# An attention factorization machine on one core: SyncE's row fetches and a placed field go, 16 tiles per quad are looked up by matmul, gathers skip ids clamped to the last row

## The reference, cut to what matters

```python
emb = jax.vmap(lambda tbl, idx: tbl[idx], in_axes=(0, 1), out_axes=1)(embed_tables, sparse)
bi = emb[:, FIRST, :] * emb[:, SECOND, :]
a = jax.nn.relu(jnp.einsum('bpd,dh->bph', bi, att_w_w) + att_w_b)
scores = jnp.einsum('bph,ho->bpo', a, att_d_w) + att_d_b
att_weight = jax.nn.softmax(scores, axis=1)
att_out = jnp.sum(att_weight * bi, axis=1)
out = jax.nn.sigmoid(jnp.concatenate([att_out, dense], axis=-1) @ fin_w + fin_b)
```

## Time and profile before

| what | value |
|---|---|
| time, median of 3 runs | 478.24 us (478.12 to 480.02) |
| span of the profiled execution | 755.4 us |
| PE busy / instructions | 489.4 us / 2788 |
| DVE busy / instructions | 419.0 us / 692 |
| ACT busy / instructions | 118.3 us / 218 |
| POOL busy / instructions | 343.8 us / 357 |
| TensorE clock granted, mean | 0.837 |

### The profile page before, as it was taken

How to read it: one execution, slowest core, us unless ns; L and a number is a source line. 1 busy time by engine, 2 the same in 40 slices (tenths; PEclk the granted TensorE clock), 3 DMA queues, 4 the chain that set the end, 5 groups by cost and what they waited for, 6 DMA issues and landing times.

```text
span 755.4 us, 9968 instructions
## 1 busy us (share of the span) xinstructions
PE 489.4 (65%) x2788; PEld 175.7 (23%) x2788; DVE 419.0 (55%) x692; ACT 118.3 (16%) x218; POOL 343.8 (46%) x357
## 2 busy tenths in 40 slices
PE   2853102136686888737696898647687989999516
PEld 0321000012222233312232233212222224433102
DVE  6943003047475656444485666254476666899616
ACT  4211000003011123000011132000012132013114
POOL 6777777624745441744564541744564640000000
PEclk9985555559888899958898999868898999999958
DMA  7532521201211111111221110121221210000000
GB/s 234 120 18 13 99 13 12 13 3 9 13 8 12 8 10 33 12 8 10 11 11 10 10 10 4 13 37 9 11 12 9 12 10 2 2 2 2 0 1 1
DMA packets 15495, 15.60 MB, mean 21 GB/s; under 512 B 8177, under 2 KB 14161, under 8 KB 15057
## 3 DMA queue, kind: packets, MB, share of 16 engines
q0 software_dynamic: 11296, 5.81, 14.3%
q1 hardware_dynamic: 3488, 8.38, 3.1%
q10 hardware_dynamic: 656, 0.79, 0.4%
HBM read 14.93 MB, written 0.02 MB: 20 GB/s over the span
## 4 chain that ended last, share of the span: by engine, by line
SPq 59%; issue 38%; DVE 1%; PE 1%; DMA 1%; ACT 1%; ACTq 0%
SPq L411 51%; SPq L407 7%; DMA index<-look_index 0%; PE sums_s L515 0%; DVE ring L855 0%; PE sums_f L501 0%; PE first L491 0%; ACT score L685 0%; SPq L380 0%; DVE neg_max_early L891 0%; DMA emb_placed<-tables 0%; SPq L385 0%; ACT second_s L627 0%; ACT hidden L614 0%; PE back_s L538 0%
## 5 line engine op out<-in xcount | busy, mean ns | idle before, releaser
L441 POOL DMA_INDIRECT emb<-tables,rows x308 | 294.0, 955 | 261.0 <-DVE emb_t L831 164.6
L476 PE MATMUL looked_own<-look_parts,onehot 128*128 128x448 bf16 x735 | 178.8, 388 | 119.3 <-issue 75.3
L855 DVE TENSOR_TENSOR ring<-emb_t,turned 128x512 f32<-128x512 f32 (+9 forms) x180 | 193.9, 1114 | 3.4
L476 PE MATMUL back_s<-look_parts,onehot 128*128 128x448 bf16 x441 | 100.5, 380 | 73.2 <-issue 49.7
L614 ACT ACTIVATE hidden<-first,par 128x512 f32<-128x512 f32 (+1 forms) x84 | 56.4, 677 | 507.8 <-PE first L491 304.6
L476 PEld LDWEIGHTS looked_own<-look_parts,onehot 128*128 128x128 bf16 x735 | 72.7, 104 | 229.4 <-issue 158.9
L491 PE MATMUL first<-ring,par 128*32 128x512 f32 (+1 forms) x672 | 105.7, 616 | 22.6 <-DVE ring L855 8.2
L501 PE MATMUL sums_f<-ring,par 128*32 128x512 f32 (+1 forms) x672 | 105.7, 605 | 5.1 <-issue 4.2
L840 DVE TENSOR_TENSOR look_masked<-back_s,look_mask 128x448 f32<-128x448 f32 x21 | 13.0, 621 | 125.0 <-remote 70.8
L750 DVE TENSOR_TENSOR onehot<-chunk_of,turned 128x2048 bf16<-128x2048 f16 (+3 forms) x30 | 53.0, 1767 | 43.0 <-PE looked_own L476 26.4
L476 PEld LDWEIGHTS back_s<-look_parts,onehot 128*128 128x128 bf16 x441 | 43.6, 103 | 137.6 <-issue 79.8
(11 more groups left out here) (71 smaller groups left out, 145.0 us busy)
## 6 DMA issues: line engine op xcount, KB each, us to landing
emb_placed<-tables SPq DMA_DIRECT2D x896, 0.1 KB
emb<-tables,rows POOLq DMA_INDIRECT x308
ring<-tables SPq DMA_DIRECT2D x3, 1568.0 KB
chunk_of<-chunk_numbers SPq DMA_DIRECT2D x3, 512.0 KB, 3.6
ring<-tables SPq DMA_DIRECT2D x1, 896.0 KB
emb<-tables,rows_first POOLq DMA_INDIRECT x44
ring<-tables SPq DMA_DIRECT2D x1, 672.0 KB
chunk_of<-chunk_numbers ACTq DMA_DIRECT2D x1, 384.0 KB, 3.9
```

What stands on the lines that cost most here:

```text
L441: pool.indirect_dma_start(emb[:, f, g * D:(g + 1) * D], None, stacked, bass.IndirectOffsetOnAxis(ap=row, axis=0), element_offset=at,).then ...
L476: mm = nc.tensor.matmul(looked_rows[look_bank[tile]], onehot[:, c, g * P:(g + 1) * P], look_parts[:, n, c, k, :], start=c == 0 and k == 0, ...
L855: nc.vector.tensor_tensor(slot[:, at:at + n, :], emb_t[:, i:i + n, :], turned[:, f % 2, :].unsqueeze(1).broadcast_to((P, n, P)), ALU.mult) ...
```

## The change

SP fetches no rows any more: `emb_placed`, the ids for it, its three DVE instructions and ACT's copy go. Field 24 is gathered like the others. All four fields in `LOOK` are looked up in all four tiles: 16 tiles a quad. POOL still issues 352 gathers, one fewer than before. SP loads the last row of each table, broadcast to all partitions (`last_rows`), ahead of the tables. For quad 0 from field 13 on and for all later quads ACT first fills the whole slot of a gathered field with the table's last row (`fill_with_last`). Ids clamped to the last row get `FAR_ROW` = 2^20 added, and the gather has a bound above which it leaves an id out. The gather now waits for the fill, which waits for DVE's transposition of the quad before.

```diff
-LOOK_TILES = (4, 4, 4, 2)
+LOOK_TILES = (4, 4, 4, 4)
-STEP_FIELDS = (1, 2, 2, 3, 4, 4, 5, 6, 6, 7, 8, *range(8, 21), 22, 24)
+STEP_FIELDS = (1, 2, 2, 3, 4, 4, 5, 6, 6, 7, 8, 8, 9, 9, 10, 11, 11, 12, 13, 13, 14, 15, 15, 16, 17, 18, 19, 20, 22, 24)
+FAR_ROW = 2 ** 20
...
+    def fills(q, f):
+        return gathers_of(f) > 0 and (q > 0 or f >= FIRST_FIELDS)
...
@@ sync
-            sp.dma_start(sp_ids[:], sp_index).then_inc(sp_ids_in, 16)
+            sp.dma_start(last_rows[:], tables[:, V - 1, :].unsqueeze(0).broadcast_to((P, F, D))).then_inc(last_rows_in, 16)
...
-                        for k in range(ROWS_SP):
-                            sp.dma_start(emb_placed[p + k:p + k + 1, q, i * D:(i + 1) * D],
-                                         stacked[bass.ds(at[k], 1), :]).then_inc(sp_gathered[tiles], 16)
+            sp.wait_ge(look_low_made[0], len(STEPS))
+            load_table(2)
+            sp.wait_ge(chunk_numbers_home, 16)
+            load_chunks(1)
+            sp.wait_ge(look_low_made[1], len(STEPS))
+            load_table(3)
+            for q in range(2, QUADS):
+                load_chunks(q)
@@ gpsimd
-                    if q and gathers_of(f):
-                        pool.wait_ge(transposed, (q - 1) * F + f + 1)
+                    if fills(q, f):
+                        pool.wait_ge(filled, fills_through(q, f))
...
-                            element_offset=at,
+                            element_offset=at, bounds_check=F * V - 1, oob_is_err=False,
@@ scalar
+            def fill_with_last(of, f):
+                if of:
+                    act.wait_ge(transposed, (of - 1) * F + f + 1)
+                nc.scalar.activation(emb[:, f, :].rearrange("p (g d) -> p g d", d=D),
+                                     last_rows[:, f, :].unsqueeze(1).broadcast_to((P, G, D)), ACT.Copy).then_inc(filled, 1)
+
+            act.wait_ge(last_rows_in, 16)
+            for f in range(F):
+                if fills(0, f):
+                    fill_with_last(0, f)
             for q in range(QUADS):
...
+                if q < QUADS - 1:
+                    fill_with_last(q + 1, 0)
                 for f in range(1, F):
-                    if f == SP_PLACE:
-                        place_rows()
...
                     for gr in done:
                         relu_group(gr)
...
+                    if q < QUADS - 1 and fills(q + 1, f):
+                        fill_with_last(q + 1, f)
@@ vector
+            nc.vector.tensor_scalar(far, clamped[:], float(V - 1), float(FAR_ROW), ALU.is_ge, ALU.mult
+                                    ).then_inc(rows_steps, 1)
+            dve.wait_ge(rows_steps, 6)
+            nc.vector.tensor_tensor(far, far, wrap, ALU.add).then_inc(rows_steps, 1)
+            dve.wait_ge(rows_steps, 7)
+            nc.vector.tensor_tensor(rows[:], moved, far, ALU.add).then_inc(rows_ready, 1)
```

More of the change, by code:

```diff
@@ L45, in layout, with attention_fm @@
     return cols, at
[L48 removed]
+def attention_fm(nc, dense, sparse, tables, params, look_index, chunk_numbers, out):
     f32, i32, bf16 = mybir.dt.float32, mybir.dt.int32, mybir.dt.bfloat16
@@ L128, in gathers_of @@
             return G - LOOK_TILES[LOOK.index(f)]
[L129 to L133, removed]
+        return G
     assert G * D == P and B % (P * G) == 0 and RING < GROUPS and 1 < END_GROUPS
@@ L151, in pieces_through_group, with fills_through @@
         return sum(1 for piece in pieces if piece[1] < (g + 1) * PAIRS_G)
+    def fills(q, f):
+        return gathers_of(f) > 0 and (q > 0 or f >= FIRST_FIELDS)
+    def fills_through(q, f):
+        return sum(1 for of in range(q + 1) for field in range(F if of < q else f + 1) if fills(of, field))
     def groups_of(f):
@@ L278, in attention_fm @@
         rows_ready = sem("rows_ready")
[L279 to L284, removed]
+        last_rows_in = sem("last_rows_in")
+        filled = sem("filled")
         gathered = [sem(f"gathered{f}") for f in range(F)]
@@ L389, in _ @@
             load_table(1)
[L391 to L397, removed]
-                    for p in range(0, P, ROWS_SP):
-                        if tiles == 0 and p == P // 4:
-                            sp.wait_ge(look_low_made[0], len(STEPS))
-                            load_table(2)
-                            sp.wait_ge(chunk_numbers_home, 16)
-                            load_chunks(1)
-                        if tiles == 0 and p == P // 2:
-                            sp.wait_ge(look_low_made[1], len(STEPS))
-                            load_table(3)
-                        _, at = nc.values_load_multi_w_load_instructions(
-                            sp_rows[t:t + 1, p:p + ROWS_SP], engines=(mybir.EngineType.SP,), min_val=0,
-                            max_val=F * V - 1, skip_runtime_bounds_check_because="rows are clamped to their table")
-                        for k in range(ROWS_SP):
-                            sp.dma_start(emb_placed[p + k:p + k + 1, q, i * D:(i + 1) * D],
-                                         stacked[bass.ds(at[k], 1), :]).then_inc(sp_gathered[tiles], 16)
-                    tiles += 1
+            sp.wait_ge(look_low_made[0], len(STEPS))
[6 more added lines that the diff above has]
+                load_chunks(q)
             sp.wait_ge(prob_done, 1)
```

39 lines of the change are left out of this document (2 added, 37 removed).

## The result

The changed kernel takes **508.97 us** (median of 4 runs, 507.49 to 509.63) against 478.58 us (478.12 to 480.02) for the kernel before in the same session: 1.0617 times as long, with a 95% interval of 1.0587 to 1.0646. The forecast was 494 us in a range of 480 to 509. Direction and bound came as forecast; the 30.4 us are nearly twice the 15.8 that were forecast, and the time lies at the very edge of the range.

The account below looks back on a forecast made before the run. POOL's and SP's chains were taken to bound the kernel at 467 to 469 us; afterwards PE's chain, 487.1, plus 9 us carried over gives 496, less some idle time 494 us (3.3% slower), range 480 to 509.

Parts of the forecast that it names:

- The chains of before: Kernel before: POOL's chain ends at 469 us, SP's at 466.6, PE with DVE's at 454.5.
- The 9 us carried over: Difference of 469 to the measured 478.24, put to time around the span and chains' mutual waiting; added unchanged to the new time.
- The chain after: PE's chain in the changed kernel, from start through the four quads to the end: 487.1 us, ending last.
- 99.6 + 14 + 4: Length of changed quad 0: DVE's work, splitting tables 2 and 3, and waits; 117.6 us.
- 3.98 a tile: PE's time for one looked-up tile; two more a quad, eight in all, add 31.8 us to PE's chain in full.
- the dearer gather: Rival, chance 0.12: a bound makes POOL's gathers cost more; 0.05 us each ties with PE, 0.1 gives 512 us.
- done by 455: Sign in the new profile: POOL is done by 455 us, or earlier if leaving rows out is cheap.
- a busy part that shrinks with the rows: POOL's gathers leaving rows out: one reading of the skill; 252 shorter gathers could save up to 208 us, covered by PE's chain.
- The load: Load of last_rows ahead of the first table on SP: delays the start by 3 us, between hidden and 6.
- no gather waited for ACT: POOL's gathers, now held by ACT's fills and relus, run far enough behind that none waits; no change in time.
- PE's idle time: Rival: PE's idle time is much smaller than thought, chain 473 to 479 us; chance 0.09 faster, 0.10 the same.
- SP's rows did not slow PE: Opposite rival, chance 0.08: SP's rows stalled PE in undisturbed runs too, 10 to 15 us; time then 485.

Follow-up runs that it names:

- experiment 5: Kernel before, without the two gathers a quad of field 19 (zeros in their place), 8 gathers fewer; 470.93 us, ratio 0.9821.
- experiment 4: Kernel before, with each of SP's 7 tiles fetched by one DMA of 128 neighbouring rows in place of 128 row DMAs; 479.5 us, ratio 1.0006.
- Experiment 9: Changed kernel with plain gathers and no skipping, DVE splitting only 32 of each 448 columns of tables 2 and 3; 497.65 us, ratio 1.0366.
- experiment 1: Kernel before with 16 looked-up tiles and the changed kernel's step places, SP still fetching its rows; 505.54 us, ratio 1.0545.
- experiment 3: Changed kernel with 14 looked-up tiles, field 19's two other tiles left as zeros, the same 352 gathers; 493.83 us, ratio 1.0301.
- experiment 6: Changed kernel without fills, far ids or last_rows load, with the bound in each gather but no id beyond it; 504.98 us, ratio 1.0526.
- experiment 8: Changed kernel with the last_rows load behind tables 0 and 1, and quad 1's fills of fields 0 to 10 held until behind quad 0's field 10; 506.7 us.
- experiment 7: Changed kernel with the load of last_rows moved behind those of tables 0 and 1; 507.33 us, ratio 1.0568.
- experiment 2: Changed kernel without its skipping: no bound, far ids, fills or load of last_rows; 504.25 us, ratio 1.0526.

## Why the prediction came out as it did

**The chains of before.** POOL was last, as forecast, at 476.8 and not at 469. The last gather starts at 456.9 (forecast 452.6): POOL is busy for 13.6 us more than 353 gathers of 0.945, in gathers stretched as in the earlier trace rows, and the 341.9 of the earlier trace rows held 9.3 of them. Landing and the wait behind it take 4.5 us, where I took 2 from one row of SP's. PE's chain ended at 469.0 (experiment 5), not at 454.5: quad 0 took 125.7 for a forecast of 113, and quad 1 took 106.6 for 104.3. SP's chain was hidden (experiment 4), as forecast; where its rows are fetched undisturbed, in experiment 5, the last one is issued by 444.4 us, and the forecast had it in at 444.7.

**The 9 us carried over.** This step was wrong. The term stood for chains waiting for one another and for time around the span. Only 2 us lie around the span; the rest was POOL's chain, undersized by 8, and so belonged to a chain that the change puts out of the way. Carried over, it made up by luck for 4.9 of the 19.9 us by which the new chain was short.

**The chain after.** Term by term against the forecast of 487.1: start 40.2 for 41.6 (-1.4); quad 0 134.1 for 117.6 (+16.5); quads 1 and 2 230.3 for 224.6 (+5.7); quad 3 to field 25 88.1 for 88.9 (-0.8). Together 507.0, 19.9 more. Of the 6.9 us that the 494 had on top of 487.1, 2.0 are there (-4.9). The balance is the 15 us by which the forecast is low.

**The step that failed is the size of quad 0.** "99.6 + 14 + 4" is DVE's work and a guess at waits. DVE's work is 117.9 for 113.6, as two more one-hots than in quad 1 fall into this quad (4.1 us), and the 4 us of waits are 16.2. So the waits are 12.2 of the 16.5 us. The sum took one engine's work where two engines of nearly equal work alternate: PE is busy for 121.2 and DVE for 117.9 of 134.1 us. PE's busy time alone is above the 117.6 of the forecast, which put it at 108.3: it makes 354 look-up matmuls between the two fields 0, where a quad has 336, and 6.4 us are the lower clock, which the forecast left out for quad 0. PE's 12.9 us of idle time end nearly all with DVE's one-hots and masks. Experiment 9 shows that DVE's splitting has 6 of the excess. The rest has no run of its own. A lack of tiles looked up ahead explains little of it: PE has made 84 look-up matmuls (4 tiles) when field 0 of quad 0 is transposed, and is 102 ahead at that of quad 1.

**The two tiles.** "3.98 a tile" from one step of the earlier trace rows is low: 8.5 us for two in quad 1, and 34.3 for eight over the program (469.0 to 503.3, experiments 5 and 1), where 31.8 was forecast. Size, not mechanism. It explains 1.1 of the +5.7 of quads 1 and 2; the other 4.6 are in the quad of 14 tiles already, which takes 106.6 for 104.3, with PE busy for 103.9 where 100.3 were counted.

**From 476.8 to 507.0.** PE's chain lay 7.8 us below POOL's, which hides as much; the tiles add 34.3; without SP's rows the span is 1.9 less; the skipping adds 5.6. The last two are differences of single profiles; 2.0 and 2.7 us of them stand in quad 0, where the clock was 0.95 with SP's rows, 0.97 without them, and 0.95 again with the skipping. Set against the forecast's own difference: PE's chain grew by 38.0 us where 32.6 were forecast, the cover under POOL's chain was 7.8 where I had 14.5, and I took off 2 at the end. Quad 0 is in both: undersized by 12.7 us in the kernel before, it made the cover too large, and undersized by 16.5 after, it made the new chain too short. That 508.97 still lies within the range is in part luck: its upper edge was drawn for a gather dearer by 0.1 us, whose own sum is 512 and not 509, and not for a longer quad 0.

**The skipping.** It gained nothing. Leaving out rows doesn't shorten a gather on POOL, and the bound makes it 0.05 us dearer. That is just the point at which I had the dearer gather tie with PE's chain, and it is why POOL was not "done by 455" but at 476. This rival had the mechanism; it didn't decide, as PE's chain ended at 507 and POOL's would have at 492 (experiment 3). The Trainium skill's "DMA: Bandwidth & Descriptors", section "SWDGE vs HWDGE vs iDMA", has a Q7 core compute descriptors for each operation, and the prediction drew from it a busy part that shrinks with the rows; experiment 6 shows none that shrinks (1003 and 1008 ns, with 11264 packets in both).

**Start and fills.** The load cost 0.9 to 2.1 us in the start (experiments 8 and 7; I took 3), DVE's two passes and the rest 0.9 to 2.1 (I took 1). The 6 us that I set as the upper bound of the load are a wrong sum: 208 pieces an engine at 0.48 us are 100 us, and I divided by the 16 engines twice. Fills take 302 ns each, for 0.3. The profile puts six gathers, 1.8 us in all, down to waiting for a fill, but that is 0.3 us each, the gap that every gather has; in experiment 2 seven such gaps stand behind DVE's transposition. So no gather waited for ACT, as forecast. The remaining 2.7 us of the skipping are in quad 0 and go with PE's clock (0.95 against 0.97). They are not shown to come from the skipping: experiment 1 has 0.95 without fills, experiment 8, which moved the fills, kept 0.95, and the runs of one kernel differ as much. What makes the clock fall once more in some executions stays open.

**The other rivals.** PE's idle time was larger than I thought in quad 0, 12.9 us, and not smaller; in quads 1 and 2 it was 3.4 each. SP's rows did not slow PE measurably: quad 1 takes 115.1 us with them and 115.2 without (experiments 1 and 2).

## What to carry to other kernels

Where two engines alternate with nearly equal work, a stage can be longer than either one's work (here 134.1 us for 121.2 and 117.9): take its length from such a stage, not from a sum of one engine's instructions. A profile whose span is far from the time can be replaced by that of a near copy of the kernel. An engine busy for 73% was the bound before, where the two others were at 88 and 89%: what counts is whose chain ends last. Before work is moved off a hidden queue onto the engine next to being the bound, measure how far below the bound that engine's chain lies, by taking away the bound's work.

## What the runs showed of the hardware

- An indirect DMA with a bound costs POOL 0.05 us more, and one that leaves out most of its rows no less (952, 1003 and 1008 ns); bytes and landing shrink (5.79 to 2.28 MB, 3.4 to 2.3 us).
- A gather on POOL is held until a DVE instruction with two SBUF inputs that began before it is over: it takes 2.63 us beside instructions of 1792 columns, 1.38 us beside those of 448. In experiment 4 all nine gathers of over 1.2 us began beside a split; the 149 that began beside DVE's products, one input of which is in PSUM, take at most 0.95. The Trainium skill's "SBUF — State Buffer", section "Who interferes with whom", says that a DVE instruction with two SBUF inputs contends with a GpSimd instruction that reads SBUF. The rows agree, and show it for the gather, which reads its ids there. Which part of the gather is held, the reading of ids or the making of descriptors, no run here separates.
- 896 single-row DMAs and their register loads on SP cost nothing that shows in the time (ratio 1.0006 without them). One profiled execution with them was stretched to 755.4 us, PE included, and three others with the same 896 were not (503.3, 469.0 and 471.2 us), so the stretching is a property of that execution and not of the rows alone.
